# A query projection taken out of attention: its own stage of seven block products, with the turned queries kept in DRAM

## The chip, the cores and the metric

The program runs on one core of one Trainium2 chip. The metric is the device time of one execution in microseconds. Three executions of the kernel before took 3114.38 to 3117.19 us, median 3116.89 us.

## What is computed

Four blocks run in turn over 2048 tokens of width 1024, each adding a gated update to x. In the first and the third, keys and values come from ctx. The change concerns the third, grouped-query attention with 32 query heads and 8 key/value heads of width 128, over 8 sequences of 256 tokens, and it touches the end of the second, which hands over x:

```python
x = x + tanh(g_xattn[0]) * autocorrelation(layernorm(x), ctx, ctx)      # 8 heads, FFTs
x = x + tanh(g_ffn[0]) * ffn_lora(layernorm(x), W, b, A, B, gate_w, gate_b)
x = x + tanh(g_xattn[1]) * gqa(layernorm(x), ctx, ctx, mask, wq, wk, wv, wo)
x = x + tanh(g_ffn[1]) * ffn(layernorm(x), W_base, b_base, enc0, enc1, coefs0, ...)

def gqa(query, key, value, mask, wq, wk, wv, wo):
    q = _rope((query @ wq).reshape(bs, s, 32, 128).transpose(0, 2, 1, 3))   # 1024 -> 4096
    k = _rope((key @ wk)...)                                                # 8 heads
    v = (value @ wv)...
    w = softmax(where(mask, q k / sqrt(128), -1e9))                         # 4 query heads per k
    return (w v) @ wo                                                       # 4096 -> 1024

def _rope(x):      # over the 128 numbers of a head, by token position
    rot = concatenate([-x[..., 64:], x[..., :64]], axis=-1)
    return x * cos + rot * sin
```

All of it is float32.

## The kernel before

**Stages.** kv makes keys and values (until about 378 us), ac is the autocorrelation block (until about 750), f0 the first feed-forward block (until about 1035), att the grouped-query attention (until about 2922), f1 the second feed-forward block. `weave` interleaves the ends and beginnings of neighbours. The order on each engine is the order in which the code is written. A gate puts semaphore waits ahead of an instruction. Nothing reorders anything.

**A float32 product** is three TensorE matmuls in fp32r (`three`, L147 to L152): every factor is held as a high part, a rounded cast made by ScalarE (ACT), and a low part, the difference from it, made by VectorE (DVE) or GpSimd (POOL). The three are high by high, high by low and low by high, so a factor costs one cast and one subtraction before it can be used.

**f0** goes over 16 tiles of 128 tokens, in pairs: layernorm, transpose, product, LoRA part, and `leave`, which adds the update into x. SP stores the finished rows in DRAM (xd), from where attention reads them again.

**att** goes over four quarters of 512 tokens, and within a quarter over 32 units u (NU = 128), one head for 512 tokens each. Before a quarter its four row tiles are loaded, normalised and transposed (`stats`, `rows`, `flip`) into at_hh and at_hl, the high and low parts of x. These flips stand between the last units of the quarter before. A unit runs on TensorE as follows:

- `scores(u)`: keys by queries, 12 matmuls 128x256. DVE takes each row's maximum with the mask bias (L2240), ACT the exponential (L2138), DVE divides (`weigh`, L2251 and L2254).
- `project(u+2)`: the query projection two heads ahead, 8 blocks of 128 rows by three, so 24 matmuls 128x512 into one bank. DVE turns it out of that bank (rope, L2222 to L2226, four operations) into at_t1, ACT casts it (L2131, at_qh), DVE makes the low part (`rest`, L2230, at_ql).
- `turn(u-1)`: eight transposes of the weights (L2058), which ACT and DVE split (L2148, L2260).
- `output`: two of the eight chunks of the group of four heads before, 24 matmuls 128x512 by wo, added into at_xt (L2274).
- `values`: weights by values, 6 matmuls 128x512.

In the first quarter the splits of wq and of wo are made: SP fetches a piece (at_rawq, at_rawo, one buffer each), ACT casts, POOL or DVE makes the low part, and SP writes both to DRAM (wqd, wod). Later quarters load the splits.

The mask of a quarter is turned into a bias by `bias` on DVE (L2198 to L2212), in unit 25 of the quarter before.

## Time and profile before

| | |
|---|---|
| median of three executions | 3116.89 us |
| profiled execution | 3115.62 us |
| its span, first to last instruction | 3113.8 us |
| mean granted TensorE clock | 0.996 |
| TensorE (PE) busy | 3072.3 us, 99%, 15136 matmuls |
| VectorE (DVE) busy | 1949.3 us, 63% |
| ScalarE (ACT) busy | 1140.8 us, 37% |
| GpSimd (POOL) busy | 700.6 us, 22% |
| DMA moved | 509 MB, 164 GB/s |

Engine shares are averages over stages with different limits. The matmuls are pipelined and their records overlap: a matmul 128x512 is listed with 0.39 us, while the next starts 0.23 us later, so the cost of one is read from start to start. Likewise a DVE operation listed with 0.69 us lets an independent one start 0.60 us after it. In listings of the trace the number before the engine is the duration; what stands in square brackets is how long the engine had been idle before and which instruction ended that.

### The profile page before, as it was taken

Reading aid. Unit: us, or ns where it says so; the run is one execution under the profiler, and the core shown is the slowest. Engines: PE = TensorE matmul, PEld = TensorE weight load, DVE = VectorE, ACT = ScalarE, POOL = GpSimd, SP = SyncE. Lnnn points to the kernel's source line nnn. Section 1 sums busy time; section 2 is a strip of 40 time slices with the busy share of each in tenths; the row PEclk is TensorE's granted clock in tenths of the full one; section 3 lists DMA queues with packets and bytes.
Section 4 is the critical chain, followed back from the end, with each engine's and each line's share of the span. In section 5 each row is a group of like instructions: output and inputs, shape, how many; then the busy total and the mean of one; then the engine's idle time right before and its main releaser. Section 6 shows DMA issues by size and latency. Waiting matters only on the chain.

```text
span 3113.8 us, 40170 instructions
## 1 busy us (share of the span) xinstructions
PE 3072.3 (99%) x15136; PEld 2571.3 (83%) x15136; DVE 1949.3 (63%) x4650; ACT 1140.8 (37%) x2382; POOL 700.6 (22%) x576
## 2 busy tenths in 40 slices
PE   9999999999999899999999999999999999999999
PEld 7888778887778788888888888888888888888887
DVE  4333488887563777778666667666667666666432
ACT  4111466665222344445333334333333333333320
POOL 2422389885322133333000000000000000000231
PEclk9999999999999999999999999999999999999999
DMA  7332412114363567777655454455455454453621
GB/s 244 129 119 99 161 52 82 48 55 170 109 223 129 198 216 238 235 250 248 224 198 175 151 182 175 163 207 173 149 186 186 162 203 161 151 176 120 252 95 55
DMA packets 232861, 509.47 MB, mean 164 GB/s; under 512 B 23180, under 2 KB 58124, under 8 KB 232668
## 3 DMA queue, kind: packets, MB, share of 16 engines
q1 hardware_dynamic: 231948, 505.45, 47.5%
q8 instruction: 121, 1.98, 0.3%
q10 hardware_dynamic: 720, 1.44, 0.1%
q14 instruction: 72, 0.59, 0.1%
HBM read 364.23 MB, written 142.61 MB: 163 GB/s over the span
## 4 chain that ended last, share of the span: by engine, by line
PE 88%; DVE 4%; ACT 3%; POOL 3%; DMA 1%; issue 0%; SPq 0%; ACTq 0%
PE PB L150 27%; PE PB L151 27%; PE PB L152 27%; PE PB L2058 3%; PE PB L640 2%; POOL ac_paw L999 1%; POOL ac_cl L982 1%; ACT ac_w L723 0%; DVE ac_st L837 0%; PE PB L2464 0%; DMA wqd<-at_wql 0%; PE PB L1235 0%; ACT ac_w L764 0%; DMA at_rawo<-in_wo 0%; PE PB L2018 0%
## 5 line engine op out<-in xcount | busy, mean ns | idle before, releaser
L150 PE MATMUL PB<-at_woh,at_ah 128*128 128x512 f32 x1024 | 409.7, 400 | 1.8 <-ACT at_pth L2148 1.8
L2138 ACT ACTIVATE at_ss<-at_ss,at_sm,at_bs 128x256 f32<-128x256 f32 x512 | 301.7, 590 | 294.8 <-DVE at_sm L2244 294.8
L150 PE MATMUL PB<-at_hh,at_wqh 128*128 128x512 f32 x1024 | 401.1, 392 | 0.6 <-DVE at_hl L2185 0.6
L151 PE MATMUL PB<-at_hl,at_wqh 128*128 128x512 f32 x1024 | 400.6, 391 | 0.0
L152 PE MATMUL PB<-at_hh,at_wql 128*128 128x512 f32 x1024 | 399.5, 390 | 0.0
L151 PE MATMUL PB<-at_wol,at_ah 128*128 128x512 f32 x1024 | 399.2, 390 | 0.0
L152 PE MATMUL PB<-at_woh,at_al 128*128 128x512 f32 x1024 | 399.1, 390 | 0.0
L2222 DVE TENSOR_TENSOR at_t<-PB,at_rt 128x512 f32<-128x512 f32 x128 | 88.4, 691 | 434.2 <-PE PB L152 434.2
L2274 DVE SCALAR_TENSOR_TENSOR at_xt<-PB,gt,at_xt 128x512 f32<-128x512 f32 x256 | 190.7, 746 | 128.0 <-PE PB L152 127.9
L2155 ACT ACTIVATE at_ah<-PB 128x512 fp32r<-128x512 f32 x128 | 76.5, 598 | 472.0 <-PE PB L152 472.0
L152 PEld LDWEIGHTS PB<-at_hh,at_wql 128*128 128x128 f32 x1024 | 192.7, 188 | 41.2
L152 PEld LDWEIGHTS PB<-at_woh,at_al 128*128 128x128 f32 x1024 | 192.2, 188 | 40.5
L150 PEld LDWEIGHTS PB<-at_hh,at_wqh 128*128 128x128 f32 x1024 | 193.3, 189 | 38.4 <-issue 1.5
L150 PEld LDWEIGHTS PB<-at_woh,at_ah 128*128 128x128 f32 x1024 | 192.5, 188 | 38.1 <-ACT at_pth L2148 2.0
L151 PEld LDWEIGHTS PB<-at_hl,at_wqh 128*128 128x128 f32 x1024 | 193.3, 189 | 35.5
L151 PEld LDWEIGHTS PB<-at_wol,at_ah 128*128 128x128 f32 x1024 | 192.8, 188 | 35.5
L2284 POOL TENSOR_SCALAR at_st<-at_st 128x1 f32<-128x1 f32 x16 | 3.5, 217 | 926.5 <-DVE at_st L2179 926.3
L2148 ACT ACTIVATE at_pth<-PB 128x512 fp32r<-128x512 f32 x256 | 138.7, 594 | 174.6 <-PE PB L2058 174.6
L2240 DVE CUSTOM_DVE_ANT_0 at_ss<-PB,at_bi 128x256 f32<-128x256 f32 x512 | 185.2, 417 | 0.0
L2260 DVE TENSOR_TENSOR at_ptl<-PB,at_pth 128x512 fp32r<-128x512 f32 x256 | 164.1, 682 | 11.8 <-ACT at_pth L2148 11.8
L2131 ACT ACTIVATE at_qh<-at_t 128x512 fp32r<-128x512 f32 x128 | 80.9, 632 | 224.5 <-DVE at_t L2226 224.5
L150 PE MATMUL PB<-at_kh,at_qh 128*128 128x256 f32 x512 | 145.7, 285 | 10.5 <-DVE at_sm L2251 7.1
(269 smaller groups left out, 7166.2 us busy)
## 6 DMA issues: line engine op xcount, KB each, us to landing
at_wqh<-wqd SPq DMA_DIRECT2D x96, 512.0 KB, 3.7
at_wql<-wqd SPq DMA_DIRECT2D x96, 512.0 KB, 4.5
at_woh<-wod SPq DMA_DIRECT2D x48, 1024.0 KB, 5.1
at_wol<-wod SPq DMA_DIRECT2D x48, 1024.0 KB, 7.5
at_rawq<-in_wq SPq DMA_DIRECT2D x32, 512.0 KB, 5.7
wqd<-at_wqh SPq DMA_DIRECT2D x32, 512.0 KB, 6.2
wqd<-at_wql SPq DMA_DIRECT2D x32, 512.0 KB, 7.3
at_rawo<-in_wo SPq DMA_DIRECT2D x32, 512.0 KB, 6.0
```

Of the source, the lines that this page charges most:

```text
L150: pe.matmul(o, ah, bh, start=start, stop=False)
L151: pe.matmul(o, ah, bl, start=False, stop=False)
L152: return pe.matmul(o, al, bh, start=False, stop=stop)
L2058: m = pe.transpose(PB[1][:, 512 * k + P * c:512 * k + P * c + P], at_ss[:, s, c, P * k:P * k + P], idt[:, :])
L2131: self.act.activation(at_qh[j][:, :], at_t1[:, :], ACT.Copy).then_inc(*inc("at_act", ("q", n)))
L2138: m = act.activation(at_ss[:, s, c, :], at_ss[:, s, c, :], ACT.Exp, bias=z[:, 4 + c:5 + c], scale=at_bs[:, qn % 2, 8 + 2 * b + c % 2:9 + 2 ...
L2148: self.act.activation(at_pth[:, k, :], BK[2 + k], ACT.Copy).then_inc(*inc("at_act", ("pt", u, k)))
L2155: self.act.activation(at_ah[:, n % 2, 2 * hp:2 * hp + 2, L * b:L * b + L], BK[at_bank.get(("values", u), 4)].rearrange("p (j n) -> p j n", ...
L2222: dve.tensor_tensor(at_t1[:, :], b, at_rt[:, 0, :], ALU.mult)
L2240: dve.tensor_tensor_reduce(out=at_ss[:, s, c, :], in0=PB[0][:, L * c:L * c + L], in1=at_bi[:, qn % 2, 2 * b + c % 2, :], scale=1.0, scalar ...
L2260: self.dve.tensor_tensor(at_ptl[:, k, :], BK[2 + k], asf(at_pth[:, k, :]), ALU.subtract).then_inc(*inc("at_dve", ("pt", u, k)))
L2274: self.dve.scalar_tensor_tensor(out=xt, in0=BK[6 + p % 2], scalar=gt[:, 2:3], in1=xt, op0=ALU.mult, op1=ALU.add).then_inc(*inc("at_dve", ( ...
```

## The change

**f0** also makes the layernorm of its own results (`stats2` on DVE, `norm2` on POOL, `rows2` on ACT), transposes them (`turn` on PE and ACT, 8 transposes per tile) and stores them turned in DRAM (xtd). Attention's own loads, layernorms and flips are gone. The number of transposes of x stays 128.

**A new stage qp** stands between f0 and att. It goes over two super-blocks (sb) of 1024 tokens and 16 pairs of heads in each. A pair is a product of 1024 rows of x^T by 256 columns of wq for 1024 tokens, cut in two along each of the three dimensions. The Strassen-Winograd form makes the four blocks of the result from seven products instead of eight. Each product is 4 chunks by three, 12 matmuls 128x512, so a pair is 84, and all 32 pairs are 2688. Before, all projections were 128 times 24, 3072.

- `expand`: for each of the four chunks g, once in a super-block, the seven token factors: ACT 7 casts, DVE 4 differences and 5 low parts, POOL 2 low parts.
- `prepare`: for each pair the seven weight factors: POOL 4 sums or differences and 7 low parts, ACT 7 casts.
- `sum`: ACT copies the first product, DVE adds the others in 7 operations.
- `turn`: the rope, 12 DVE operations 128x512. A head is spread over two block rows, so that both inputs of each lie in SBUF.
- SP fetches 1 MB of wq for a pair and stores 1 MB of turned queries (qd). It reads wq twice in all and caches no split of it.

The first pair of a super-block is done by chunks (`chunk`): seven products over chunk 0, then over chunk 1, and so on, as the expansions come. All others are done product by product.

**att** loses `project` and the rope. `fetch_q` loads 256 KB for a unit four units ahead, `split_q` casts it on ACT and makes the low part on POOL. The loop is three units deep (at_ss has 3 slots), output follows its group by five units, and `split_wo` starts a unit later. The buffers of f1 lie elsewhere, and seven of its eight weight loads are issued at unit NU-12.

```diff
@@ weave: what of qp stands within f0's last tiles (yields of f0_schedule)
             for t in f0:
-                if t in (4, 6, -8, 8, "half", 10, 12, None):
-                    next(att)
+                if t in (12, "begin", "odd", "rows", "turn"):
+                    next(qp)
+            next(att)
+            next(qp)
+            next(att)
+            for _ in qp:
+                pass
@@ qp_schedule
+            for sb in range(2):
+                first = NP * sb
+                do.fetch_w(first + 2)
+                if sb:
+                    do.expand(1, 0)
+                    for i in range(4, 7):
+                        do.sum(first - 1, i)
+                for g in range(4):
+                    if g:
+                        do.expand(sb, g)
+                    if g == 2 and sb:
+                        do.turn(first - 1)
+                    if g + 2 < 4:
+                        do.fetch_x(sb, g + 2)
+                    do.chunk(first, g)
+                    if g < 2:
+                        do.prepare(first + 1, g)
...
+                for i in range(7):
+                    do.sum(first, i)
+                do.turn(first)
+                for i in range(2, 7):
+                    do.prepare(first + 1, i)
+                for pair in range(first + 1, first + NP):
...
+                    for i in range(7):
+                        do.product(pair, i)
+                        if pair != NP - 1 or i < 4:
+                            do.sum(pair, i)
+                        if pair + 1 < 2 * NP:
+                            do.prepare(pair + 1, i)
+                    if pair != NP - 1:
+                        do.turn(pair)
@@ the rope of a pair, on DVE; t stands for 512 tokens, top and low for halves of two heads
+                for tn in range(2):
...
+                    dve.tensor_tensor(q0, top, qp_angle(0), ALU.mult).then_inc(*inc("qp_dve", ("cos", pair, tn)))
+                    dve.tensor_tensor(q1, top, qp_angle(1), ALU.mult).then_inc(*inc("qp_dve", ("top", pair, tn)))
...
+                    dve.tensor_tensor(t, low, qp_angle(1), ALU.mult).then_inc(*inc("qp_dve", ("t", pair, tn)))
+                    on.wait_ge(*at("qp_dve", ("t", pair, tn)))
+                    dve.tensor_tensor(low, low, qp_angle(0), ALU.mult).then_inc(*inc("qp_dve", ("low", pair, tn)))
+                    dve.tensor_tensor(q0, q0, t, ALU.subtract).then_inc(*inc("qp_dve", ("q0", pair, tn)))
+                    on.wait_ge(*at("qp_dve", ("low", pair, tn)))
+                    dve.tensor_tensor(q1, q1, low, ALU.add).then_inc(*inc("qp_dve", ("q1", pair, tn)))
@@ the low part of a weight factor, on POOL
+            def low(self, pair, i):
...
+                self.pool.tensor_tensor(qp_part(j, 1), qp_weight(pair, i), asf(qp_part(j, 0)), ALU.subtract).then_inc(
+                    *inc("qp_pool", ("w", pair, i)))
@@ at_schedule, the loop over units, without the loads, take and bias
+            for u in range(NU + 5):
...
+                if 2 <= u < NU + 2:
+                    do.turn(u - 2)
+                if u < NU:
+                    do.scores(u)
+                if more and w == 25:
+                    do.bias(qn + 1)
+                if u + 2 < NU:
+                    do.split_q(u + 2)
+                    if u + 4 < NU:
+                        do.fetch_q(u + 4)
+                m, k = (u - 5) // 4, (u - 5) % 4
+                if u > 4:
+                    do.output(m, 2 * k)
+                if 1 <= u < NU + 1:
+                    do.weigh(u - 1)
+                if 2 <= u < NU + 2:
+                    do.values(u - 2)
+                if u > 4:
+                    do.output(m, 2 * k + 1)
+                do.split_wo(u)
```

On VectorE, in the middle of attention, a unit before held the rope and the query's low part; at_t is the query being turned, at_rt the angles, PB a PSUM bank, and the line numbers are those of the kernel before:

```order
L2222 TENSOR_TENSOR at_t_185<-PB,at_rt 128x512
L2223 TENSOR_TENSOR at_t_186<-PB,at_rt 64x512
L2224 TENSOR_TENSOR at_t_186<-PB,at_rt 64x512
L2226 TENSOR_TENSOR at_t_185<-at_t_185,at_t_186 128x512
L2260 TENSOR_TENSOR at_ptl<-PB,at_pth 128x512 x2
L2230 TENSOR_TENSOR at_ql_184<-at_t_185,at_qh_181 128x512
```

In the changed kernel a pair of the query stage holds on VectorE its last sums and then its rope, with lines of the changed kernel; qp_c are the four blocks of the result, qp_r the turned halves, qp_t a temporary:

```order
L2162 TENSOR_TENSOR qp_c_197<-qp_c_197,PB 128x512
L2162 TENSOR_TENSOR qp_c_199<-qp_c_199,PB 128x512
L2162 TENSOR_TENSOR qp_c_198<-qp_c_198,PB 128x512
L2194 TENSOR_TENSOR qp_r_202<-qp_c_197,qp_rope 128x512
L2195 TENSOR_TENSOR qp_r_203<-qp_c_197,qp_rope 128x512
L2198 TENSOR_TENSOR qp_t<-qp_c_199,qp_rope 128x512
L2200 TENSOR_TENSOR qp_c_199<-qp_c_199,qp_rope 128x512
L2201 TENSOR_TENSOR qp_r_202<-qp_r_202,qp_t 128x512
L2203 TENSOR_TENSOR qp_r_203<-qp_r_203,qp_c_199 128x512
L2194 TENSOR_TENSOR qp_r_204<-qp_c_198,qp_rope 128x512
```

The rope, half of which read PSUM, now reads SBUF alone, and it stands as one block of 12 behind the sums of a pair.

On GpSimd, in the first quarter of attention, there stood before one split for wo and one for wq in a unit:

```order
L2303 TENSOR_TENSOR at_wol<-at_rawo,at_woh 128x1024
L2295 TENSOR_TENSOR at_wql_159<-at_rawq,at_wqh_157 128x1024
```

In the changed kernel this is GpSimd's work for one pair of the query stage (qp_raw the fetched weights, qp_s a sum, qp_a the ring of factors):

```order
L2225 TENSOR_TENSOR qp_s_196<-qp_raw_191 128x512
L2227 TENSOR_TENSOR qp_raw_191<-qp_raw_191 128x4x2x64
L2212 TENSOR_TENSOR qp_a_159<-qp_raw_191,qp_a_159 128x512
L2231 TENSOR_TENSOR qp_raw_191<-qp_s_196,qp_raw_191 128x4x2x64
L2212 TENSOR_TENSOR qp_a_160<-qp_raw_191,qp_a_160 128x512
L2212 TENSOR_TENSOR qp_a_161<-qp_raw_191,qp_a_161 128x512
L2212 TENSOR_TENSOR qp_a_162<-qp_s_196,qp_a_162 128x512
L2212 TENSOR_TENSOR qp_a_154<-qp_raw_191,qp_a_154 128x512
L2235 TENSOR_TENSOR qp_raw_191<-qp_raw_191 128x4x2x64
L2212 TENSOR_TENSOR qp_a_155<-qp_raw_191,qp_a_155 128x512
L2212 TENSOR_TENSOR qp_a_156<-qp_raw_191,qp_a_156 128x512
```

So eleven operations 128x512 with both inputs in SBUF, in each of 32 pairs, stand beside the twelve of VectorE.

## Rows read from the trace of the kernel before

**Rows 1.** The page: busy time, share and instructions; then the chain's shares.

```profile
PE 3072.3 (99%) x15136; PEld 2571.3 (83%) x15136; DVE 1949.3 (63%) x4650; ACT 1140.8 (37%) x2382; POOL 700.6 (22%) x576
...
PE 88%; DVE 4%; ACT 3%; POOL 3%; DMA 1%; issue 0%; SPq 0%; ACTq 0%
```

**Rows 2.** Windows: stretch, length, busy PE, PEld, DVE, ACT, POOL; clock, DMA, GB/s.

```profile
20.00:120.00 100.00, 100.00 (x443) 82.81 (x442) 48.80 (x70) 30.99 (x50) 32.15 (x25) 1.00 0.51 170
400.00:700.00 300.00, 296.39 (x1471) 247.22 (x1472) 255.04 (x672) 200.28 (x371) 262.95 (x204) 0.99 0.18 61
760.00:1000.00 240.00, 237.74 (x1151) 187.63 (x1151) 127.11 (x304) 67.63 (x90) 66.45 (x75) 1.00 0.46 159
1040.00:1050.00 10.00, 4.42 (x25) 3.47 (x23) 6.39 (x18) 3.50 (x9) 0.00 (x0) 0.85 0.56 185
1050.00:1060.00 10.00, 8.46 (x29) 7.05 (x30) 5.85 (x19) 5.11 (x12) 0.00 (x0) 0.64 1.01 307
1070.00:1080.00 10.00, 6.75 (x40) 5.78 (x40) 8.44 (x24) 6.54 (x14) 2.41 (x1) 1.00 0.75 270
1080.00:1090.00 10.00, 8.16 (x41) 6.64 (x40) 8.29 (x19) 4.42 (x12) 0.00 (x0) 1.00 1.01 328
2000.00:2400.00 400.00, 400.00 (x2032) 339.89 (x2031) 263.90 (x672) 135.48 (x338) 3.12 (x9) 1.00 0.52 176
```

**Rows 3.** Timeline of TensorE over one unit in steady attention.

```profile
2003.30 1.03 PE L2058 MATMUL PB<-idt,at_ss 128*128 128x128 f32 x8
...
2012.42 0.40 PE L150 MATMUL PB<-at_hh,at_wqh 128*128 128x512 f32 x1
...
2017.90 1.03 PE L2058 MATMUL PB<-idt,at_ss 128*128 128x128 f32 x8
```

**Rows 4.** Timeline of VectorE in the same unit: rope's last operation and the next.

```profile
2005.63 0.69 DVE L2226 TENSOR_TENSOR at_t<-at_t,at_t 128x512 f32<-128x512 f32 x1
2006.24 1.28 DVE L2260 TENSOR_TENSOR at_ptl<-PB,at_pth 128x512 fp32r<-128x512 f32 x2
```

**Rows 5.** Groups of instructions by form: busy time, mean ns; idle before them.

```profile
L2131 ACT ACTIVATE at_qh<-at_t 128x512 fp32r<-128x512 f32 x128 | 80.9, 632 | 224.5 <-DVE at_t L2226 224.5
L2303 POOL TENSOR_TENSOR at_wol<-at_rawo,at_woh 128x1024 fp32r<-128x1024 f32 x32 | 77.2, 2411 | 341.8 <-ACT at_woh L2165 341.8
```

**Rows 6.** Timeline near 756 and 744 us: GpSimd and VectorE, both inputs in SBUF.

```profile
755.88 2.41 POOL L1658 TENSOR_TENSOR f0wl<-f0raw,f0wh 128x1024 fp32r<-128x1024 f32 x1 [9.90 <-ACT f0wh L1337]
756.78 2.58 DVE L1474 TENSOR_TENSOR f0wl<-f0raw,f0wh 128x1024 fp32r<-128x1024 f32 x1 [1.09 <-ACT f0wh L1337]
761.58 1.23 DVE L1474 TENSOR_TENSOR f0wl<-f0raw,f0wh 128x1024 fp32r<-128x1024 f32 x1 [2.22 <-ACT f0wh L1337]
...
743.02 2.96 POOL L999 TENSOR_TENSOR ac_paw<-ac_paw,ac_pbw 128x512 f32<-128x512 f32 x2
743.31 0.68 DVE L902 TENSOR_TENSOR ac_pbw<-PB,ac_kk 128x512 f32<-128x512 f32 x1
743.90 0.94 DVE L909 TENSOR_TENSOR ac_slw<-ac_paw,ac_shw 128x512 fp32r<-128x512 f32 x1
744.25 1.73 POOL L999 TENSOR_TENSOR ac_paw<-ac_paw,ac_pbw 128x512 f32<-128x512 f32 x1
744.76 1.77 DVE L909 TENSOR_TENSOR ac_slw<-ac_paw,ac_shw 128x512 fp32r<-128x512 f32 x1
```

**Rows 7.** A piece of wo in the first quarter: its cast, and two landings.

```profile
L2165 ACT ACTIVATE at_woh<-at_rawo x1: 1051/1051/1051, 1210.8 to 1210.8; 128x1024 fp32r<-128x1024 f32 x1
...
DMA to landing us min/median/max: 3.6/3.6/3.6
...
DMA to landing us min/median/max: 8.2/8.2/8.2
```

**Rows 8.** Timeline of VectorE: first operation of a bias, and the next maximum.

```profile
1386.64 0.68 DVE L2198 TENSOR_SCALAR at_bi<-at_bi 128x1024 f32<-128x1024 f32 x1
...
1393.29 0.42 DVE L2240 CUSTOM_DVE_ANT_0 at_ss<-PB,at_bi 128x256 f32<-128x256 f32 x1
```

More of the change, by code:

```diff
@@ L1280, in mid @@
             def mid(t):
-                product(t, 1, range(C))
+                product(t, 1, range(4))
+                turn(t - 1, 0)
+                turn(t - 1, 1)
+                product(t, 1, range(4, C))
                 add_lora(t)
@@ L1593, in first_end @@
                 stats(5)
+                stats2(0)
+                stats2(1)
             def begin(t):
@@ L1813, in f0_sync @@
             yield
-            yield from f0_schedule(first_begin, first_chunk, first_end, begin, mid, lambda t: piece(2 * t + 2), end)
+            yield from f0_schedule(first_begin, first_chunk, first_end, begin, mid, odd, end, lambda: None,
+                                   lambda hf: store_turned(NT - 1) if hf else None)
+        NP = H // 2
+        Q_BANK = (0, 1, 4, 5, 6, 7, 2, 3)
+        Q_READY = (0, 4, 6, 3, 1, 2, 5)
+        NR = 9
+        qp_ring = [place(f"qp_a{i}", kb, [P, 2, 4, P], R) for i, kb in enumerate((52, 64, 60, 187, 191, 195, 0, 68, 72))]
@@ L1907, in at_schedule @@
-            do.fetch_wq(3)
-            do.bias(0)
+                do.fetch_q(n)
+            for n in range(2):
+                do.split_q(n)
+                do.fetch_q(n + 2)
             yield
-            do.split_wq(3)
-            for u in range(NU + 4):
-                n, k, qn, w = u // 4, u % 4, u // 32, u % 32
+            for u in range(NU + 5):
+                qn, w = u // 32, u % 32
                 more = qn + 1 < NQ
-                late, last, new = w == 30 and more, w == 31 and more, w == 0 and 0 < u < NU
-                plain = not late and not last
-                do.fetch_ahead(u)
-                if u == NU - 2:
-                    yield
-                if w in (3, 4) and 0 < qn < NQ:
-                    do.take(qn, 2 * w - 6)
-                    do.take(qn, 2 * w - 5)
+                if u == NU - 12:
+                    yield
+                if w in (4, 5) and 0 < qn < NQ:
+                    do.take(qn, 2 * w - 8)
+                    do.take(qn, 2 * w - 7)
+                do.fetch_ahead(u)
```

763 lines of the change are left out of this document (442 added, 321 removed).

## The prediction

> **What bounds the kernel now.** I read the page first. TensorE is busy 99% of the span and holds 88% of the chain that ended last; VectorE is at 63%, GpSimd at 22% [rows 1]. So the kernel is bound by matmuls nearly everywhere, and removing matmuls gains their full time, but only as long as nothing else becomes late. Then the windows [rows 2]: 443 matmuls in 100 us without a gap give **0.2257 us** each. From 2000 to 2400 TensorE is never idle, while VectorE works 263.9 of 400 us. Added up over windows from 1100 to 2890 us, only 2.9 us are lost. The start of attention is the exception: from 1040 to 1060 and from 1070 to 1090 the busy times fall short by 5.58 + 1.54 + 3.25 + 1.84 = 12.2 us, and the granted clock of 0.85 and 0.64 costs 0.15 x 4.42 + 0.36 x 8.46 = 3.7 us more. A unit lasts 2017.90 - 2003.30 = 14.60 us, of which the query projection has 2017.90 - 2012.42 = 5.48 [rows 3].
>
> **What goes.** 128 projections at 5.48 are 701.4 us. In their place stand 2688 matmuls at 0.2257, 606.7. That is **-94.7**, all on the path. The old start goes (-15.9) and the 2.9 of idle time, so **-113.5**. The flips of x move and cost the same. The splits of wq (GpSimd, SP) go, off the path. The later waits are those of VectorE: what it does in a unit is 263.9 x 14.6 / 400 = 9.6 us, less five operations of the projection (0.6 to 0.7 each, 3.4), so 6.2, against 14.60 - 5.48 = 9.12 of matmuls. By hand its chain through a unit comes to 7.9. I take the steady unit as bound by matmuls, with 1.2 us of cover.
>
> **The query stage.** The time of a pair is the largest of three.
> TensorE: 84 x 0.2257 = **18.96 us**.
> VectorE: 7 sums and 12 rope operations. One follows another after 0.61 us (2005.63 to 2006.24 [rows 4]) or 0.71 where it needs its result, so about 0.65: 4.6 and 7.8, together 12.4. Alone it would be hidden.
> GpSimd: 11 operations 128x512. A 128x1024 takes 2.41 [rows 5], so 1.2 each, 13.2. Alone it would be hidden as well.
> But the two don't run side by side where both read two inputs from SBUF. GpSimd's subtraction runs from 755.88 to 758.29. VectorE's, begun at 756.78, takes 2.58 us where the same one takes 1.23 with GpSimd idle: it ends 1.07 us after GpSimd does [rows 6]. At 744 both have such work queued and they alternate: VectorE's ends are at 744.84 and 746.53, a cycle of **1.69 us**, in which 0.61 is its own and 1.08 is GpSimd's. A VectorE operation with an input in PSUM (L902) keeps its 0.68 while GpSimd runs [rows 6]. So the seven sums are free of this, and the twelve rope operations, which now have both inputs in SBUF, aren't.
> Of GpSimd's eleven some run during the sums and while VectorE waits for TensorE; those cost nothing. GpSimd is behind (its ring lets it run at most two factors ahead), so it has work queued during the rope. If nothing else ran, 12 rope operations and N of GpSimd's alternate. VectorE's time is 12.4 + 1.08 N. With its 4.6 us of sums, and the same again of waiting for the products that they need, GpSimd gets rid of three to four operations, which leaves N = 7.3 to 8.1: 20.3 to 21.2 us. I take 21.0, **+2.0 in each of 30 pairs, +61**. The lower end is the use of the port alone, 12 x 0.61 + 11 x 1.08 = 19.2, so 0.3 a pair, +10; the upper end is all eleven alternating, 12.4 + 11.9 = 24.3, so +160. The sums of a pair wait for its products and then TensorE waits for the banks: eight banks hold one product more than a pair has, so VectorE being late by 2 us reaches TensorE within the next pair.
>
> The Trainium skill describes this ("SBUF — State Buffer", Terms and "SBUF: two separate sides"): GpSimd and VectorE share a port pair under an exclusive lock, taken by a VectorE operation with two SBUF inputs and held for a whole instruction. The trace agrees, with 2.58 for 1.23. By the rule the sum of both engines' port times is a floor, so a pair could not be shorter than 19.2 to 20.3 us; without it a pair would take 18.96 and the sum would be 61 us lower.
>
> **The ramp from f0.** The last f0 tile must be added, normalised (by way of GpSimd), cast, transposed and only then can the last chunks' products follow. For a chunk VectorE has nine operations, and between them waits for three casts of 0.63 [rows 5] whose factors it needs: 9 x 0.65 + 3 x 0.95 = 8.7, with the casts' starts and the landing of the next chunk about 10.6. TensorE needs 21 x 0.2257 = 4.74 per chunk. Four chunks lose 4 x 5.9 = 23, and the last tile's own chain about 5: **+28.4** (15 to 45). f0's added work lies beside its matmuls (VectorE is busy 127 of 240 us there [rows 2]), +1. GpSimd's weights for two pairs stand in the same stretch, and about eight of its operations push VectorE's by 1.08: **+8**.
>
> **The change of super-blocks.** VectorE expands four chunks (8.0 each) and has the rope of pair 15 (7.8) between the second and the third: 39.8 against 4 x 4.74 = 19: **+21** (10 to 30).
>
> **The new start of attention.** The rope of pair 31 (7.8) stands on VectorE ahead of the first maximum. Then five units run without outputs, with 9.12 - 5.48 = 3.6 us of matmuls against VectorE's 7.9, so 21.5. Less a little for what overlaps: **+28** (15 to 40).
>
> **The bias.** It holds VectorE for 1393.29 - 1386.64 = 6.65 us [rows 8]. Before, 5 us of spare VectorE time per unit covered it. Now a unit has 9.12 - 7.9 = 1.2, two units' slack and the depth of three take about half: 3 x 3.4 = **+10** (0 to 20).
>
> **wo's splits.** In the first quarter a piece lands, is cast (1.05) and split (2.41), then the next is fetched into the same buffer, every second one behind two stores: 3.6 + 8.2 + 2 x 3.46 + 0.7 of waking and issue = 19.4 us for two units [rows 5, 7]. Two units used to last 29.2 and will last 18.2, so this chain binds: 14 x 1.16 = **+16** (5 to 30; less if the landings shorten with the wq traffic gone).
>
> **The clock.** Before, 12.2 us of gaps came with 3.7 us of lower clock (0.50 to 0.85 granted). Now there are three ramps with some 80 us of gaps: **+12** (3 to 25).
>
> **Sum:** -113.5 + 61 + 28.4 + 1 + 8 + 21 + 28 + 10 + 16 + 12 = +72, rounded; 3115.6 + 72 = 3188 for a profiled execution. The median stood 1.3 above that: **3189 us**, 2.3% slower.
>
> **Rivals.**
> *The port costs nothing* (2 in 10). GpSimd's work falls into the sums and VectorE's waits, a pair stays at 18.96 us, and only the ramps and attention's new edges eat the gain: 3189 - 61 = 3128, or about 3115 if the pieces of wo don't bind. For it: both engines have over 5 us a pair to spare, and from 400 to 700 us both are busy 85% and 88% while TensorE keeps its 99% [rows 2]. Against it: the rope is one block of 12 with nothing from PSUM in between, and GpSimd's queue isn't empty then.
> *Faster* (1.5 in 10). The mechanism is the depth of the pipelines: the three edges are 28 + 21 + 28 = 77 us in my sum because I let no chain overlap another. If, besides a free port, they come to half and wo's chain and the bias stay hidden in the deeper loop, the total is -113.5 + 39 + 9 + 5 = -60: 3056. It decides at a pair below 19.8 us together with edges below half: then the result is under 3100. For it speaks that the first chunk's work is put into f0's last two tiles, where VectorE has 47% of its time free.
> *All of GpSimd's operations alternate* (1 in 10). Each rope operation finds GpSimd ahead, 24.3 us a pair: +160 for +61, 3289. For it: GpSimd waits for the port as well, so its work is pushed out of the sums into the next rope. Against it: 24.3 leaves time for it to catch up.
> *The change doesn't do what it says*: ruled out, as the products are 2688 for 3072 in the built program.
> A fifth, that attention's steady unit is bound by VectorE (GpSimd's query split, 1.2 us each, may hold it up), would add at most 120 x 0.5 = 60 and lies within the range.
>
> **How the numbers follow.** Forecast (port-bound query stage, 20.0 to 22.0 a pair, edges as summed): 0.55, giving 3150 to 3240. Port free: 0.2, 3100 to 3150. Faster: 0.15, 3040 to 3100. All alternate: 0.1, above 3240. A range from 3085 to 3250 leaves out the last case and most of the faster one, 2 in 10. A measurement of this kernel can tell about 0.2% (6 us) from no change: 3111 to 3123 is "same". Of the port-free case a third falls there and a tenth below it. So faster 0.19, same 0.07, slower 0.74.
>
> **What would show it.** In the query stage the first matmul of a pair comes every 21 us (18.96 if I am wrong), VectorE's rope operations (first 0.65 apart) stand 1.0 to 1.7 us apart, GpSimd's listed durations rise from 1.2 to about 1.7, and TensorE waits before products for VectorE's sums. Windows of f0's end, the middle of the query stage and attention's first 60 us show 28, 21 and 28 us of idle time on TensorE. In the first quarter TensorE waits for wo or GpSimd at every second unit; in later quarters a unit lasts 9.12 us. The prediction is wrong if a pair takes under 19.3 us, or if a steady unit lasts over 9.5.

## The result, and the profile after

The changed kernel takes 3202.93 us (median of four, 3201.76 to 3204.15) against 3116.29 of the kernel before: a ratio of 1.0279, 95% interval 1.0261 to 1.0297. The forecast was 3189. Its page, with the same lines as [rows 1]:

```profile
PE 3029.0 (95%) x14752; PEld 2519.9 (79%) x14752; DVE 2195.1 (69%) x4654; ACT 1261.7 (39%) x2662; POOL 1366.9 (43%) x1044
...
PE 58%; DVE 15%; POOL 11%; DMA 8%; ACT 6%; issue 2%; SPq 0%; DVEq 0%; POOLq 0%; ACTq 0%
```

TensorE does 384 matmuls fewer and is busy 43 us less, but its share of the chain falls from 88% to 58%; VectorE, GpSimd, DMA and ScalarE hold most of the rest. Windows over the stages show where this happens (columns as in [rows 2]):

```profile
1020.00:1100.00 80.00, 53.73 (x187) 39.28 (x188) 44.50 (x53) 29.96 (x51) 39.01 (x33) 0.81 0.30 107
1160.00:1400.00 240.00, 227.62 (x986) 185.10 (x984) 236.29 (x226) 52.35 (x93) 198.56 (x128) 0.99 0.40 105
1400.00:1480.00 80.00, 45.36 (x160) 32.59 (x159) 69.80 (x75) 25.70 (x47) 47.06 (x31) 0.79 0.29 79
1480.00:1760.00 280.00, 268.19 (x1163) 219.23 (x1162) 275.63 (x263) 60.29 (x107) 232.50 (x150) 0.99 0.40 105
1760.00:1840.00 80.00, 50.69 (x228) 42.16 (x228) 51.62 (x149) 34.01 (x85) 18.87 (x13) 0.74 0.56 165
1840.00:2120.00 280.00, 265.66 (x1438) 227.06 (x1437) 193.41 (x556) 158.52 (x375) 105.95 (x57) 1.00 0.65 219
2160.00:2560.00 400.00, 399.29 (x2186) 344.46 (x2185) 276.74 (x841) 197.93 (x523) 55.78 (x43) 1.00 0.59 185
```

These are the ramp, the pairs of the first super-block, the change of super-blocks, the pairs of the second, the start of attention, its first quarter, and a steady stretch. Summed over windows of 10 us through the traces, the difference between the two profiled spans (3200.0 - 3113.8 = 86.2 us) is made of three parts:

| us | before | after | difference |
|---|---|---|---|
| TensorE idle | 41.5 | 171.0 | +129.5 |
| busy time at a lower granted clock (busy x (1 - clock)) | 9.1 | 41.6 | +32.5 |
| busy time apart from that | 3063.2 | 2987.4 | -75.8 |

The idle time by stage:

| stage | before | after |
|---|---|---|
| f0, 740 to 1000 us | 6.0 | 13.3 |
| ramp into the query stage, 1000 to 1100 | | 27.5 |
| pairs, 1100 to 1400 and 1480 to 1760 | | 24.2 |
| change of super-blocks, 1400 to 1480 | | 34.6 |
| start of attention | 12.2 | 29.3 |
| first quarter's rest, 1840 to 2120 | 2.9 for both | 14.3 |
| later quarters, to 2960 | | 3.0 |
| the end | 3.9 | 8.9 |

(Before, attention starts within 1000 to 1100, and 2.9 is its whole stretch from 1100 to 2890 us. The rest, kv and ac, is 16 us in both.)

In the query stage VectorE is busy 236.29 of 240 us. This is one pair's rope on VectorE and the GpSimd operations beside it:

```profile
1165.01 0.69 DVE L2194 TENSOR_TENSOR qp_r<-qp_c,qp_rope 128x512 f32<-128x512 f32 x1
1165.62 0.69 DVE L2195 TENSOR_TENSOR qp_r<-qp_c,qp_rope 128x512 f32<-128x512 f32 x1
...
1167.55 1.78 DVE L2201 TENSOR_TENSOR qp_r<-qp_r,qp_t 128x512 f32<-128x512 f32 x1
1169.25 1.77 DVE L2203 TENSOR_TENSOR qp_r<-qp_r,qp_c 128x512 f32<-128x512 f32 x1
1170.95 1.78 DVE L2194 TENSOR_TENSOR qp_r<-qp_c,qp_rope 128x512 f32<-128x512 f32 x1
...
1168.86 1.62 POOL L2227 TENSOR_TENSOR qp_raw<-qp_raw 128x512 f32<-128x512 f32 x1
1170.44 1.74 POOL L2212 TENSOR_TENSOR qp_a<-qp_raw,qp_a 128x512 fp32r<-128x512 f32 x1
```

The first operations stand 0.61 us apart. GpSimd's begin at 1167.49 once its weights have landed, and from there both alternate at 1.70 us, as in [rows 6]. (Of the rope's four operations in the kernel before, three read PSUM, L2222 to L2224, and only L2226 had both inputs in SBUF.) The sums, which read PSUM, keep their length. From one pair to the next the block of seven stands at

```profile
1160.33 4.64 DVE L2162 TENSOR_TENSOR qp_c<-qp_c,PB 128x512 f32<-128x512 f32 x7
1180.05 4.64 DVE L2162 TENSOR_TENSOR qp_c<-qp_c,PB 128x512 f32<-128x512 f32 x7
1201.14 4.65 DVE L2162 TENSOR_TENSOR qp_c<-qp_c,PB 128x512 f32<-128x512 f32 x7
1220.87 4.65 DVE L2162 TENSOR_TENSOR qp_c<-qp_c,PB 128x512 f32<-128x512 f32 x7
1241.94 4.65 DVE L2162 TENSOR_TENSOR qp_c<-qp_c,PB 128x512 f32<-128x512 f32 x7
```

so 19.7 and 21.1 us in turn, **20.40 us a pair**. Of that the sums have 4.65 and the rope the rest: VectorE has no time left over.

### The profile page after: what moved, and what is told of

Read it like the earlier page. It is cut to its first block, busy times and chain, and to the rows that moved or that the text cites. A ratio compares the mean times of both kernels' runs of the same rounds, so it can differ in the third digit from the quotient of the medians.

```text
span 3200.0 us, 40953 instructions
## 1 busy us (share of the span) xinstructions
PE 3029.0 (95%) x14752; PEld 2519.9 (79%) x14752; DVE 2195.1 (69%) x4654; ACT 1261.7 (39%) x2662; POOL 1366.9 (43%) x1044
## 4 chain that ended last, share of the span: by engine, by line
PE 58%; DVE 15%; POOL 11%; DMA 8%; ACT 6%; issue 2%; SPq 0%; DVEq 0%; POOLq 0%; ACTq 0%
PE PB L150 17%; PE PB L151 17%; PE PB L152 17%; POOL qp_a L2212 4%; DMA at_rawo<-in_wo 4%; DMA qp_raw<-in_wq 3%; PE PB L2407 3%; DVE qp_c L2162 2%; PE PB L641 2%; DVE qp_r L2203 2%; POOL at_wol L2566 1%; POOL ac_paw L1000 1%; DVE qp_c L2200 1%; DVE qp_r L2194 1%; ACT at_ss L2453 1%
## 5 line engine op out<-in xcount | busy, mean ns | idle before, releaser
L2559 POOL TENSOR_TENSOR at_ql<-at_qf,at_qh 128x512 fp32r<-128x512 f32 x128 | 166.3, 1299 | 887.3 <-ACT at_qh L2446 887.3
L150 PE MATMUL PB<-qp_b,qp_a 128*128 128x512 f32 x896 | 361.0, 403 | 78.8 <-DVE qp_b L2134 35.9
L150 PE MATMUL PB<-at_woh,at_ah 128*128 128x512 f32 x1024 | 402.8, 393 | 18.7 <-DVE at_sm L2516 8.7
L151 PE MATMUL PB<-qp_b,qp_a 128*128 128x512 f32 x896 | 355.3, 397 | 0.0
L152 PE MATMUL PB<-qp_b,qp_a 128*128 128x512 f32 x896 | 354.9, 396 | 0.0
L2212 POOL TENSOR_TENSOR qp_a<-qp_raw,qp_a 128x512 fp32r<-128x512 f32 x192 | 294.2, 1545 | 61.0 <-ACT qp_a L2090 58.5
L150 PEld LDWEIGHTS PB<-qp_b,qp_a 128*128 128x128 f32 x896 | 172.2, 192 | 134.0 <-issue 33.5
L2090 ACT ACTIVATE qp_a<-qp_raw 128x512 fp32r<-128x512 f32 x192 | 113.9, 623 | 379.1 <-POOL qp_raw L2235 185.8
L152 PEld LDWEIGHTS PB<-qp_b,qp_a 128*128 128x128 f32 x896 | 172.1, 192 | 37.0
L151 PEld LDWEIGHTS PB<-qp_b,qp_a 128*128 128x128 f32 x896 | 172.7, 193 | 34.3
L150 PE MATMUL PB<-at_kh,at_qh 128*128 128x256 f32 x512 | 157.2, 307 | 18.0 <-DVE at_sm L2516 10.0
L2530 DVE TENSOR_SCALAR at_ss<-at_ss,at_sm 128x256 f32<-128x256 f32 x512 | 161.0, 378 | 4.5
```

The lines of the kernel that those rows point to most:

```text
L150: pe.matmul(o, ah, bh, start=start, stop=False)
L151: pe.matmul(o, ah, bl, start=False, stop=False)
L152: return pe.matmul(o, al, bh, start=False, stop=stop)
L2090: self.act.activation(qp_part(j, 0), qp_weight(pair, i), ACT.Copy).then_inc(*inc("qp_act", ("w", pair, i)))
L2212: self.pool.tensor_tensor(qp_part(j, 1), qp_weight(pair, i), asf(qp_part(j, 0)), ALU.subtract).then_inc(*inc("qp_pool", ("w", pair, i)))
L2530: dve.tensor_scalar(at_ss[:, s, c, :], at_ss[:, s, c, :], z[:, 12 + c:13 + c], None, ALU.mult).then_inc(*inc("at_dve", ("weight", u, c)))
```

## Experiments

Each kernel is the changed one with the edit shown; `...` stands for lines left out. But for the two at the end each has one profiled run, so its time has no interval. Four runs of the changed kernel spread over 2.4 us and ten of one of the combined kernels over 6.8 us, so a gain of 6 or 7 us from a single run is not shown by the time alone. There the idle time of the stretch that was edited is the better witness.

**GpSimd's work made thin.** The weight factors' low parts are mostly not computed from the third pair on.

```diff
-                self.pool.tensor_tensor(qp_part(j, 1), qp_weight(pair, i), asf(qp_part(j, 0)), ALU.subtract).then_inc(
+                thin = (lambda a: a[:, 0:1, 0:1, :]) if pair > 1 else (lambda a: a)
+                self.pool.tensor_tensor(thin(qp_part(j, 1)), thin(qp_weight(pair, i)), thin(asf(qp_part(j, 0))), ALU.subtract).then_inc(
...
+                a11, a12, a21, a22, s1 = (thin(a) for a in (a11, a12, a21, a22, qp_s1_block()))
```

> GpSimd's eleven operations of a pair (sums and low parts of the weight factors) work on 64 of their 512 columns from the third pair on; all instructions and waits stay, but most of the weight factors' low parts aren't computed. Theory A (VectorE's rope waits for the port that GpSimd holds): the rope's twelve operations stand 0.61 to 0.71 us apart, a pair goes from 20.40 us to TensorE's own 19.1, 28 pairs give 36 us, and the change of super-blocks, where GpSimd's operations also stand among VectorE's, loses 5 to 10 us of its 34.6 us of idle TensorE: 3155 to 3162 us in all. Rival B (VectorE's own work and its waits for ScalarE and the products bind, the port only stretches what would be waiting anyway): a pair stays at 20.2 to 20.4 us and the time at 3195 to 3203.

Measured: 3144.9 us, 58 less, where theory A had 41 to 48. A pair takes 19.04 us. Theory A holds. Its forecast left out the start of attention, where pair 31's rope meets the same lock: the idle time there falls from 29.3 to 22.1 us and the time at a lower clock from 11.3 to 4.5. At the change of super-blocks 13.3 us came back, for the 5 to 10 that it said.

**The angles in PSUM.** This separates the port from GpSimd's own lateness, since GpSimd's work stays whole. ScalarE fills the bank once.

```diff
-        Q_BANK = (0, 1, 4, 5, 6, 7, 2, 3)
+        Q_BANK = (0, 1, 4, 5, 6, 7, 2)
...
-            return BK[Q_BANK[(7 * pair + i) % 8]]
+            return BK[Q_BANK[i]]
...
-            return qp_rope[:, k, :].unsqueeze(1).to_broadcast([P, 2, L])
+            return BK[3][:, L * k:L * k + L].unsqueeze(1).to_broadcast([P, 2, L])
...
+            def turn(self, pair):
+                if pair == 0:
+                    self.on.wait_ge(*at("qp_rope", 1))
+                    self.act.activation(BK[3].rearrange("p (k n) -> p k n", k=2), qp_rope[:, :, :], ACT.Copy).then_inc(*inc("qp_act", "angles"))
...
-                on.wait_ge(*at("qp_rope", 1))
+                on.wait_ge(*at("qp_act", "angles"))
```

> The rope's angles stand in a PSUM bank, so that 8 of its 12 operations have one input in SBUF; the products rotate over seven banks instead of eight. GpSimd's work is as in the changed kernel. Theory A: only the 4 additions meet the lock, VectorE needs 12.4 + 1.08 x 4 = 16.7 us a pair, TensorE binds again at 19.1, about 3160 us. Rival B as before: 20.4 a pair, 3200. Rival C (it is not the port but GpSimd, whose weight factors come late): GpSimd's work is unchanged, so a pair stays at 20.4 here, although the run with thin GpSimd work gets faster. If seven banks are too few, TensorE waits for VectorE's sums at each pair, which would show as waits on the first product.

Measured: 3145.6 us, 57 less. Over the pairs of the first super-block, the windows of this run and, below it, of the run with thin GpSimd work:

```profile
1100.00:1380.00 280.00, 280.00 (x1237) 231.86 (x1236) 188.12 (x283) 69.54 (x122) 226.20 (x168) 1.00 0.45 121
```

```profile
1100.00:1380.00 280.00, 280.00 (x1237) 231.86 (x1236) 191.90 (x285) 71.93 (x123) 85.74 (x168) 1.00 0.46 121
```

In both TensorE has no gap. GpSimd is busy 226.2 us in the one and 85.7 in the other, which makes no difference: rivals B and C fall. An operation that reads an angle from PSUM keeps its length (first row). So do most of the additions with both inputs in SBUF (19 of 128 take over 1.2 us). Here the first finds GpSimd waiting for ScalarE, and then GpSimd's operation is the one that waits, 1.77 us for 1.30:

```profile
1173.16 0.69 DVE L2203 TENSOR_TENSOR qp_r<-qp_c,PB 128x512 f32<-128x512 f32 x1
...
1175.69 0.68 DVE L2210 TENSOR_TENSOR qp_r<-qp_r,qp_t 128x512 f32<-128x512 f32 x1
...
1176.36 1.77 POOL L2221 TENSOR_TENSOR qp_a<-qp_raw,qp_a 128x512 fp32r<-128x512 f32 x1 [3.18 <-ACT qp_a L2094]
...
1178.21 1.30 POOL L2240 TENSOR_TENSOR qp_raw<-qp_s,qp_raw 128x512 f32<-128x512 f32 x1
```

Here too a pair takes 19.04 us (the first operations of two ropes stand at 1173.16 and 1192.20). Seven banks are enough. The change of super-blocks gains as well, since rope and GpSimd met the same lock there: its idle time is 21.5 us (60 - 38.52, window 1380 to 1440) for 34.6.

```profile
1380.00:1440.00 60.00, 38.52 (x133) 27.62 (x132) 51.06 (x63) 20.61 (x37) 29.50 (x22) 0.80 0.25 71
```

At the start of attention it is 21.5 for 29.3. Over the whole span idle time falls by 48.2 us, the time at a lower clock by 1.5, and the rest of TensorE's busy time by 6.4. Nearly all of the 6.4 lies in the products of the query stage, where fewer matmuls now start after a wait; one that does is listed with 0.47 or 0.50 us instead of 0.39.

**Two buffers for wo.**

```diff
-        at_rawo = place("at_rawo", 52, [P, D])
+        at_rawo = [place(f"at_rawo{i}", kb, [P, D]) for i, kb in enumerate((52, 60))]
...
-                before = at_half(u - 1)
+                before, last = at_half(u - 2), at_half(u - 1)
...
-                    if jj == 0 and before[0] >= 0:
-                        self.keep_wo(*before[:2])
...
+                    if jj == 0 and last[0] >= 0:
+                        self.keep_wo(*last[:2])
```

> wo's pieces of the first quarter land in two buffers in turn, and a piece is fetched ahead of the two stores instead of behind them. Theory (the chain of fetch, cast, low part and fetch of one buffer takes 19.4 us for two units and binds): TensorE's idle time from 1840 to 2120 us, 14.3 us, falls to 2 at most, 3189 to 3192 us in all. Rival (the stretch is bound by VectorE's or GpSimd's operations that hold each other up): the idle time stays above 10 and the time at 3198 to 3203.

Measured: 3184.0 us, 19 less. In the changed kernel ScalarE waited for these pieces 17 times from 1840 to 2120 us, 42.8 us in all:

```profile
ACT at_woh L2480 <- DMA at_rawo<-in_wo: 42.8, 17, 4.6
```

With two buffers that wait is gone from the list, and the window has 1.9 us of idle TensorE for 14.3:

```profile
1840.00:2120.00 280.00, 278.06 (x1516) 239.46 (x1515) 194.69 (x587) 166.03 (x398) 106.21 (x59) 1.00 0.73 238
```

The theory holds for 12.4 us. The other 6 are spread over the ramps (3.0 us less idle time at the change of super-blocks, 4.4 less at a lower clock at the start of attention), where this single run differs from the changed kernel without a cause in the edit. I leave them open.

**The start of attention, twice.** In the changed kernel the first maximum comes late for two reasons of order. SyncE stands in pair 30's stores until 1766.5 us and only then issues the first fetches of queries. ScalarE waits 14.65 us for them, with the copy of pair 31's first product queued behind:

```profile
1760.38 6.10 SPq L2285 DMA_DIRECT2D qd<-qp_r  x8
1766.60 7.12 SPq L2582 DMA_DIRECT2D at_qf<-qd  x4
...
1770.12 1.36 ACT L2446 ACTIVATE at_qh<-at_qf 128x512 fp32r<-128x512 f32 x2 [14.65 <-DMA at_qf<-qd]
1771.39 0.58 ACT L2122 ACTIVATE qp_c<-PB 128x512 f32<-128x512 f32 x1
...
1784.24 0.42 DVE L2516 CUSTOM_DVE_ANT_0 at_ss<-PB,at_bi 128x256 f32<-128x256 f32 x1
```

The edit; at the new yield stand the first two fetches of queries, and `fetch_late` loads the angles again where they don't stand in attention's way:

```diff
@@ qp_schedule
+                    if pair + 2 == 2 * NP:
+                        yield
-                    if pair != NP - 1:
+                    if pair != NP - 1 and (pair + 1 < 2 * NP or not True):
                         do.turn(pair)
+                    elif True and pair + 1 == 2 * NP:
+                        do.fetch_late()
...
@@ at_schedule
+                if u in (8, 12):
+                    do.late_turn((u - 8) // 4)
```

> The start of attention: the queries of the first units are fetched ahead of the stores of pair 30 and cast behind the copy of pair 31's first product, and the rope of pair 31 is done in units 8 and 12 with angles loaded again. Theory (the first maximum, at 1784 us, is late by 6 us of queue order on SyncE and ScalarE and by 7.4 us of the last rope): the first maximum comes 12 to 16 us sooner, 10 us come back as idle time and 2 to 4 as clock, 3188 to 3192 us. Rival (the five units without outputs are bound by VectorE's chain whatever comes first): the idle time only moves later, 3198 to 3203.

Measured: 3210.9 us, 8 *more*. The first maximum came 8 us sooner and the start had 19.1 us of idle time for 29.3, but the first quarter lost 23.5 for 14.3, and 5.5 us of clock. So I moved the late rope alone:

```diff
-                if u in (8, 12):
-                    do.late_turn((u - 8) // 4)
+                if u in (36, 44):
+                    do.late_turn((36, 44).index(u))
```

> The same start of attention as in the run before it with the last rope in units 8 and 12, but with that rope in units 36 and 44, where SyncE no longer writes and fetches pieces of wo. That run brought the first maximum 8 us forward, yet it lost 23 us instead of 14 from 1840 to 2120 us. Theory (SyncE stood in the rope's stores while the next piece of wo was due): the idle time of the first quarter goes back to 14 us and the whole gives 3192 to 3196 us. Rival (five units without outputs are bound by VectorE and by wo's pieces from the start, and an earlier start only waits longer): 3199 to 3205.

Measured: 3197.0 us, 6 less than the changed kernel, 14 less than the run with units 8 and 12. Idle time from 1840 to 2120 is 17.1 us, and its clock is back at 1.00:

```profile
1760.00:1840.00 80.00, 59.88 (x307) 50.10 (x306) 54.69 (x158) 39.50 (x98) 22.74 (x15) 0.87 0.64 203
1840.00:2120.00 280.00, 262.87 (x1416) 224.60 (x1416) 192.99 (x555) 155.62 (x370) 103.36 (x56) 1.00 0.65 219
```

The rope's place in the quarter of the wo pieces was the harm. The trace of the run with units 8 and 12 shows both ways in which it acts, here for unit 8:

```profile
1856.76 0.47 PE L150 MATMUL PB<-at_pth,at_vh 128*128 128x512 f32 x1 [1.30 <-DVE at_ptl L2557]
...
1855.44 2.41 SPq L2299 DMA_DIRECT2D qd<-qp_r  x4
...
1867.44 1.06 ACT L2498 ACTIVATE at_woh<-at_rawo 128x1024 fp32r<-128x1024 f32 x1 [5.18 <-DMA at_rawo<-in_wo]
...
1869.86 0.64 PE L150 MATMUL PB<-at_pth,at_vh 128*128 128x512 f32 x1 [2.89 <-DVE at_ptl L2557]
```

TensorE first waits 1.30 us because the rope holds VectorE. A unit later it waits 2.89 us more, because the fetch of the next piece of wo stood behind the rope's stores and ScalarE then stood at its landing. At unit 12 the same two waits are 1.28 and 3.90 us. So 6.8 us came by way of SyncE and 2.6 by way of VectorE. The rival is half right: of 9 us won at the start 3 are lost behind it.

**The change of super-blocks.** The last rope and sums of the first super-block, put where VectorE waits for casts; `between(k)` issues the next k operations of pair 15's rope.

```diff
-                    if g == 2 and sb:
-                        do.turn(first - 1)
+                    if g == 3 and sb:
+                        do.store(first - 1)
...
@@ QpVector.expand, (sb, g) = (1, 1..3)
                 dve.tensor_tensor(b11, b22, b11, ALU.subtract).then_inc(*inc("qp_dve", ("T", sb, g, 1)))
+                between(2)
...
+                between(1)
                 on.wait_ge(*at("qp_pool", ("x", sb, g, 4)))
                 dve.tensor_tensor(b21, b21, b11, ALU.subtract).then_inc(*inc("qp_dve", ("T", sb, g, 5)))
+                between(1)
...
```

> At the change of super-blocks the last three sums of pair 15 stand inside the first expansion and its rope's twelve operations in the places where VectorE waits for ScalarE's casts in the other three, instead of in one block. Theory (in this stretch VectorE's chain binds, with 1.2 + 0.8 us of waits in each expansion beside the block of 7.3 us): 5 to 8 us less, 3195 to 3198. Rival (GpSimd's lock and the reload of the factors bind, the waits are taken by them): 3201 to 3204.

Measured: 3196.7 us, 6.2 less, as the theory said; idle time is 80 - 54.21 = 25.8 us for 34.6:

```profile
1400.00:1480.00 80.00, 54.21 (x185) 39.09 (x186) 75.16 (x78) 26.10 (x47) 52.86 (x35) 0.79 0.29 82
```

**Matmuls that keep TensorE busy in the ramps.**

```diff
@@ QpTensor.chunk
+                    if g:
...
+                        for _ in range(3):
+                            self.pe.matmul(qp_bank(pair, i), qp_zero[:, :], qp_x[0][0][:, 0, :], start=False, stop=False)
                     self.ready(pair, i, g)
```

> Three matmuls 128x512 with a factor of zeros stand before each wait of the chunks 1 to 3 of both super-blocks, 126 in all, 29 us of TensorE's time put into some 55 us of its idle time. They change nothing in the result. Theory (the ramps' gaps are what lowers the granted clock, 9.5 us lost from 1000 to 1100 and 7.2 from 1400 to 1480): the clock stays at 1.0 there for the most part, the lost clock falls to 4 us, and since the stretches are bound by VectorE the time falls only by what TensorE's slow matmuls had held up, 3 to 10 us: 3193 to 3200. Rival (the lower clock was covered, since VectorE binds in the ramps): 3200 to 3206 with the granted clock higher all the same.

Measured: 3203.7 us, the same. In the first ramp the granted clock rises from 0.81 to 0.94, at the change of super-blocks it stays at 0.79:

```profile
1020.00:1100.00 80.00, 61.32 (x256) 47.51 (x257) 46.09 (x55) 30.08 (x52) 37.99 (x32) 0.94 0.28 99
1400.00:1480.00 80.00, 57.26 (x220) 45.56 (x221) 67.26 (x73) 24.82 (x44) 45.90 (x31) 0.79 0.28 79
```

In the first ramp the lower clock was covered but for 2 us at most, so the rival holds there. But the zeros weren't free. The waits of VectorE for ScalarE, in the changed kernel, here, and at the end of the second ramp here:

```profile
1086.02 0.69 DVE L2134 TENSOR_TENSOR qp_b<-qp_in,qp_b 128x512 fp32r<-128x512 f32 x1 [2.77 <-ACT qp_b L2115]
```

```profile
1084.76 0.69 DVE L2142 TENSOR_TENSOR qp_b<-qp_in,qp_b 128x512 fp32r<-128x512 f32 x1 [3.46 <-ACT qp_b L2123]
...
1461.15 0.69 DVE L2170 TENSOR_TENSOR qp_c<-qp_c,PB 128x512 f32<-128x512 f32 x1 [2.01 <-PE PB L152]
```

ScalarE's casts stand behind its copies of f0's last transposes, and these transposes stand behind a chunk's products on TensorE. So TensorE is itself a link of the chain that sets the pace. Three more matmuls, by zeros, make such a chunk 0.7 us longer (13.45 for 12.73), and 0.7 us in each of three chunks is the most that a faster clock can have given back unseen. In the second ramp the last chunk's products come so late that VectorE waits for them; there the clock didn't change, and the run says nothing of its price.

**ScalarE's order in the ramp.** In the changed kernel ScalarE stands at the weights' landing, and then at a sum of GpSimd's, while f0's work is queued behind it; TensorE and VectorE wait for that:

```profile
1018.96 0.63 ACT L2090 ACTIVATE qp_a<-qp_raw 128x512 fp32r<-128x512 f32 x1 [11.69 <-DMA qp_raw<-in_wq]
...
1025.14 0.43 DVE L1589 TENSOR_TENSOR f0at<-PB,f0at 64x256 fp32r<-64x256 f32 x1 [12.30 <-ACT f0at L1395]
...
1026.29 1.97 PE L1189 MATMUL PB<-idt,f0xn 128*128 128x128 f32 x8 [7.56 <-ACT f0xn L1362]
```

```diff
@@ qp_schedule: first casts one step of f0 later
-            do.prepare(0, 0)
-            do.prepare(0, 1)
             yield
-            for i in range(2, 5):
+            for i in range(5):
                 do.prepare(0, i)
@@ f0_schedule: last tile's layernorm behind the second chunk's casts, its copies behind the next ones
-            last_rows()
             yield "rows"
+            last_rows()
             for hf in range(2):
                 last_turn(hf)
                 yield "turn"
+                last_copy(hf)
...
```

> The ramp from f0 with ScalarE's queue in another order: the first casts of weights stand one step of f0 later, so that they don't wait 11.7 us for the weights' landing ahead of f0's own work; the second chunk's casts stand ahead of the last tile's layernorm, and the copies of that tile's transposes behind the casts of the next chunk. Theory (27.5 us of idle TensorE from 1000 to 1100 us: VectorE's chain binds, but 7.6 us at 1026 and some 3 us for each of three chunks are ScalarE standing at something else): 10 to 15 us less, 3188 to 3193. Rival (only VectorE's nine operations per chunk count, the waits before them are covered): 3199 to 3204.

Measured: 3196.0 us, 6.9 less; I had expected 10 to 15. The wait of 7.56 us is gone, and VectorE's waits between the chunks, 3.8, 2.8 and 2.8 us, fell to 0, 1.5 and 0.3. But the transposes of the next tile now wait 3.38 us, and VectorE stands 10.6 us before the first chunk:

```profile
1031.82 1.27 POOL L2234 TENSOR_TENSOR qp_raw<-qp_raw 128x512 f32<-128x512 f32 x1
...
1034.43 1.24 ACT L1363 ACTIVATE f0xn<-f0xt,f0st 128x1024 f32<-128x1024 f32 x1 [5.36 <-POOL f0st L1727]
...
1035.72 1.09 PE L1190 MATMUL PB<-idt,f0xn 128*128 128x128 f32 x8 [3.38 <-ACT f0xn L1363]
...
1037.33 0.78 DVE L2133 TENSOR_TENSOR qp_b<-qp_in,qp_b 128x512 fp32r<-128x512 f32 x1 [10.61 <-ACT qp_b L2114]
```

VectorE hands over the statistics of that tile at 1026.7 us, GpSimd works on weight factors until 1033.1 and only then on the statistics, and ScalarE stands at them 5.36 us with the first expansion's casts queued behind. In the second chunk it is the same engine: the low parts of the tokens stand behind GpSimd's work for the next pair's weights, and the chunk takes 14.9 us as before. So what is left of this ramp is in good part the order of GpSimd's queue, and no run changed that.

**All together.** First without the ramp's order:

> Angles in PSUM, two buffers for wo, the earlier start with the last rope in units 36 and 44, and the rope of pair 15 within the expansions, together. By the single runs -57 and -19 are known; if the other two give 7 and 6 as expected and all add up, 3114 us: no different from the kernel before (3110 to 3120). If the start and the change were bound by the same lock that the angles in PSUM have already taken away, they add nothing: 3124 to 3130.

Measured: 3121.4 us (3119.4 to 3126.2, ten runs), ratio to the kernel before 1.0021, interval 1.0012 to 1.0031. That lies between the two cases: 81.5 us gained, where the four single gains add up to 88.4. Then with it:

> All edits that gained by themselves and the new order of the ramp. The run without the ramp's order gave 3121.4 us. If the ramp gives its 10 to 15 us here too: 3106 to 3111 us, 0.2 to 0.3% faster than the kernel before. If the angles in PSUM had already taken away what the ramp's order saves: 3118 to 3121, slower or the same.

Measured: **3110.7 us** (3108.2 to 3112.8, eleven runs), ratio 0.9987, interval 0.9978 to 0.9996. The ramp's order gave 10.7 us here, as forecast and more than by itself. The single gains (57.3, 18.9, 6.0, 6.2, 6.9) add up to 95.3 and the whole gains 92.2. The sums fit, but that doesn't show that nothing overlaps, as 7 us were lost in the first step and 4 won in the second. So the change comes out even with the kernel before, or 0.1% ahead, once 92 us have been taken away again; the difference is less than the 6 us that the prediction counts as "same".

## Why the prediction was right, and where not

The direction and the main mechanism were right. That the time came so close (3189 for 3203) is partly luck. Sorted as in the table above, the terms of the forecast are 158 us of idle time (with the 12.2 + 2.9 that go), 8 of clock (12 less 3.7) and -95 of the rest. Measured were 129.5, 32.5 and -75.8. So the idle time was 29 us too high, the clock 24 and the rest 19 too low, and most of that cancels. Point by point:

- **The query stage bound by VectorE waiting for GpSimd's port: right, shown by two runs.** Said: 21.0 us a pair, with 7.3 to 8.1 of GpSimd's operations in between. Measured: 20.40, and the two lengths of the rope, 15.05 and 16.41 us, less 12 x 0.61, are 7.1 and 8.4 times 1.08. The term was mis-sized all the same. A pair is 0.6 us shorter than said, and TensorE's own pair is 19.04 us and not 18.96, so 1.36 us are left where I had 2.0: 41 us in 30 pairs for 61. Of these, 24 show as idle time, the others as lower clock, as matmuls that start again, and as first pairs in which TensorE still has free banks (no idle time from 1100 to 1160 us). But the lock also held up the change of super-blocks and the start, where I hadn't counted it. Taking it away gave 57 us in all, against 61 + 8 in the sum.
  The 0.2257 us of a matmul was misread: a count over a window takes in the matmuls at both of its edges. From 20 to 220 us there are 884, so the second hundred holds 441, and one takes 0.2268.
  The rule of the Trainium skill ("SBUF — State Buffer", Who interferes with whom: the lock is exclusive, and a VectorE operation with two SBUF inputs takes it against a GpSimd operation that reads SBUF) agrees: with one of the inputs in PSUM the rope's 256 multiplications all keep their 0.69 us or less.
- **What goes: -94.7 said, -75.8 measured.** 384 matmuls at 0.2268 are 87; the rest of the 94.7 is the 0.2257 above and 0.04 us in a projection's 5.48 that its 24 matmuls don't need. Of the other 11 us, 6 are matmuls of the query stage that start after a wait, which went away with the angles in PSUM. The last 5 come by order: the scores now stand right behind the transposes, where the output stood, and counted from start to start at full clock the scores take 12 us more and the output 7.5 less. This is read from the two traces; no run tested it.
- **The ramp: 28.4 + 8 said, 27.5 of idle time measured**, of which some 7 were not VectorE's chain but ScalarE standing at a DMA and at GpSimd ahead of f0's work. I had costed what the moved steps do and not what they wait for in the queue of an engine. The new order gave 6.9 us by itself and 10.7 with the other edits.
- **f0: +1 said, +7.2 measured**, half of it between 780 and 800 us (4.9 us idle for 1.2), where VectorE is busy 17.7 of 20 us and was busy 17.3 before. Its 127 of 240 us is an average over a stage with a crowded beginning. But the longest of these waits, 2.4 us, is for a layernorm on ScalarE, and no run tested the cause.
- **The change of super-blocks: +21 said, 34.6 measured.** The four expansions wait 1.2 + 0.8 us for casts in each, and the lock stretches them, as in the third:

```profile
1435.60 1.65 DVE L2140 TENSOR_TENSOR qp_in<-qp_in 128x512 f32<-128x512 f32 x1
...
1441.49 1.29 DVE L2134 TENSOR_TENSOR qp_b<-qp_in,qp_b 128x512 fp32r<-128x512 f32 x2 [1.22 <-ACT qp_b L2115]
...
1444.15 0.69 DVE L2134 TENSOR_TENSOR qp_b<-qp_in,qp_b 128x512 fp32r<-128x512 f32 x1 [0.77 <-ACT qp_b L2115]
```

  The rope in the gaps gave back 9 us of this idle time (6 us in all), the angles in PSUM 13.
- **The start of attention: +28 said, 29.3 measured, for other reasons in part.** I named the rope ahead of the first maximum; the order on SyncE and ScalarE (6 us) stood beside it.
- **The bias [rows 8]: +10 said, some 2 measured** (0.7 in each of the windows that hold the last two, at 2319 and 2613 us, and none at the one before them). That the third slot of at_ss covers it is likely, but not shown.
- **wo's splits [rows 7]: +16 said, 14.3 measured.** Right, and shown.
- **The clock: +12 less the old start's 3.7 said, +32.5 measured.** The old start had 3.7 us beside 12.2 of gaps, 0.30 for one; the three ramps have 28 beside 91, 0.31 for one. So the ratio held, and the step that failed is that I put down half of what it gives for my 80 us of gaps. But this is hardly a term that can be added: in the one ramp where the clock was brought back, nothing was won.
- **The end: 0 said, +5 measured.** 4 of it are one wait of TensorE at the end of attention, for VectorE's low part of the weights. What made VectorE late stays open.

```profile
2984.26 0.51 PE L150 MATMUL PB<-at_pth,at_vh 128*128 128x512 f32 x1 [3.96 <-DVE at_ptl L2536]
```

So there was too much for the pairs and the bias, too little for clock, f0, the change of super-blocks and the end. The rival "port free" is what the two runs without the lock give: 3145 us, 17 above the 3128 that I gave for it. "Faster" asked for a result under 3100 us and was reached by no run; with the port free and the ramps mended it is 3110.7. "All alternate" is excluded by 20.4 us a pair. The signs that I named came: 20.4 us a pair, GpSimd's operations at 1.7 us beside the rope, and a steady unit of 9.14 us.

## What to carry to other kernels

A product saved on TensorE pays only if its additions find a place. Here seven products for eight gave 87 us, and cost 12 VectorE operations with both inputs in SBUF beside 11 of GpSimd's: add up both engines' time for such operations, against TensorE's, before moving anything from PSUM to SBUF, and put a constant operand in PSUM if a bank can be spared. A new stage has ramps of its own. Cost each by what every in-order engine is queued at there, the DMA waits among it, and not by the work alone.
